# Second attention of a two-layer transformer kernel: router logits four tiles at a time with the gate matrix as weights, and the attention's gate multiplied into the projection's weights by GpSimd

## The reference

```
h  = layernorm(x) * (1 + ca) + sa                 # ca, sa, ga, cb, sb, gb: rows of 256 per batch
Q, K, V = (h @ Wq.T), (h @ Wk.T), (h @ Wv.T)      # 16 heads of 16
scores[b, s] = Q[b, s] @ K[b, s].T / 4            # 16 x 16: heads against heads of the same token
attn = softmax(scores);  o = attn @ V
x  = x + ga * (o @ Wfc.T)                         # ga: one row of 256 per batch
h  = layernorm(x) * (1 + cb) + sb
logits = h @ Wg                                   # Wg: 256 x 8 experts; then softmax, top tokens per expert
```

## Time and profile before

| | us |
|---|---|
| median of three runs | 1049.5 |
| lowest and highest run | 1048.51, 1049.79 |
| span of the profiled execution, first to last instruction | 1045.7 |
| second attention in it, first to last scores (L1713) | 553 to 777 |
| its tail until the router starts | until 822 |

### The profile page before, as it was taken

One profiled execution on the slowest core, in us unless ns is written; L12 is line 12 of the kernel. 1 busy time (PEld: TensorE's weight loads), 2 busy tenths in 40 slices (PEclk: granted clock), 3 DMA queues, 4 the chain that ended last, 5 costly groups with the idle time before them and its releaser, 6 DMA issues. The chain is left out here.

```text
span 1045.7 us, 30362 instructions
## 1 busy us (share of the span) xinstructions
PE 959.2 (92%) x11177; PEld 823.6 (79%) x11178; DVE 690.6 (66%) x1747; ACT 496.8 (48%) x1343; POOL 377.1 (36%) x330
## 2 busy tenths in 40 slices
PE   6899999889999999999987999999767888999996
PEld 3466666879999999999965778888666878899995
DVE  3478877855777777777412688889985776344442
ACT  3556665404454554554446777777552440322221
POOL 0134335521223223222213455555561101455552
PEclk9999999999999999999998899999868999999998
DMA  9885581294232222221055657766421620444441
GB/s 338 216 331 122 126 269 41 97 386 115 85 102 79 87 97 85 89 92 71 8 107 92 115 124 150 154 134 128 99 68 57 266 108 22 151 134 140 134 136 35
DMA packets 133025, 135.59 MB, mean 130 GB/s; under 512 B 73884, under 2 KB 122142, under 8 KB 130740
## 3 DMA queue, kind: packets, MB, share of 16 engines
q1 hardware_dynamic: 121684, 90.80, 31.5%
q0 software_dynamic: 11232, 43.27, 13.0%
HBM read 96.21 MB, written 44.77 MB: 135 GB/s over the span
## 5 line engine op out<-in xcount | busy, mean ns | idle before, releaser
L1151 PE MATMUL psall<-rows 128*128 128x128 f32 x1872 | 224.8, 277 | 1.6 <-issue 1.1
L1151 PEld LDWEIGHTS psall<-rows 128*128 128x128 f32 x1872 | 219.6, 194 | 3.1 <-issue 1.3
L1114 POOL DMA_INDIRECT x<-ffn_rows,tok_i x78 | 82.6, 1059 | 171.8 <-DVE tok_i L999 69.9
L1165 PE MATMUL psall<-whi,rows 128*128 x624 | 141.0, 379 | 0.0
L1244 DVE COPY rows<-wlo 128x2048 f32 (+2 forms) x78 | 74.5, 955 | 95.8 <-PE psall L1151 85.2
L1165 PEld LDWEIGHTS psall<-whi,rows 128*128 128x128 f32 x624 | 115.7, 190 | 14.1
L1119 POOL DMA_INDIRECT attn_rows<-rows,tok_i x39 | 41.7, 1070 | 183.9 <-DVE rows L1276 183.9
L1504 DVE STREAM_TRANSPOSE whi<-whi 32x512 f32<-32x512 f32 x128 | 89.7, 701 | 9.1 <-POOL whi L1467 7.7
L1584 ACT ACTIVATE whi<-psall 32x512 f32<-32x512 f32 x128 | 75.3, 588 | 30.8 <-PE psall L1713 27.3
L280 PE MATMUL psall<-cst 128*128 128x128 f32 x714 | 88.4, 280 | 0.5 <-PEq L1387 0.5
L1306 ACT ACTIVATE rows<-psall,vs 128x128 f32<-128x128 f32 x312 | 85.0, 383 | 4.4 <-PE psall L1151 2.1
(11 more groups left out here) (250 smaller groups left out, 1731.3 us busy)
## 6 DMA issues: line engine op xcount, KB each, us to landing
ffn_rows<-mod_rows SPq DMA_DIRECT2D x2, 4096.0 KB
wlo<-in_W SPq DMA_DIRECT2D x2, 4096.0 KB, 17.5
whi<-in_w SPq DMA_DIRECT2D x5, 1024.0 KB
whi<-mod_rows SPq DMA_DIRECT2D x4, 1024.0 KB, 15.0
ffn_rows<-rows SPq DMA_DIRECT2D x8, 512.0 KB
ffn_rows<-x SPq DMA_DIRECT2D x8, 512.0 KB
wlo<-attn_rows SPq DMA_DIRECT2D x32, 128.0 KB, 3.4
v_turn<-wlo SPq DMA_DIRECT2D x32, 128.0 KB, 2.6
```

Source lines behind the costliest of these rows:

```text
L1114: eng.indirect_dma_start(xin[j % DEEP], None, src_d, bass.IndirectOffsetOnAxis(tok_i[:, j:j + 1].bitcast(U32), 0), bounds_check=T, oob_is_ ...
L1151: last = eng.matmul(b_up[t.par][f // 4][:, (f % 4) * P:(f % 4 + 1) * P], w_now[:, c, f * P:(f + 1) * P], inT[t.par][:, c * P:(c + 1) * P], ...
L1165: last = eng.matmul(b_dn[t.par][:, 0:D], hidT[t.par][:, f * P:(f + 1) * P], w_down[:, bass.ds(e, 1), f, :].rearrange("p o n -> p (o n)"), ...
```

## The change

Logits: for all tiles but the last four, the logits are no longer computed tile by tile. When the four tiles of a batch have been turned, group_logits computes them with Wg as weights (8 columns wide, each tile in its own column group of the array) and the turned tiles moving; the result has experts as rows. ScalarE copies it in four pieces, TensorE turns it in the next step (turn_logits), and ScalarE copies it to where the router reads (keep_group_logits).

Gate: GpSimd multiplies `wfc` by the batch's row ga into a second copy `wfc_g`, in three parts in the three steps after the projection of the batch before (gate_weights). project uses `wfc_g` and waits for the parts by the semaphore `pre`. VectorE then adds its result to x for four tiles in one instruction; gate_attention, yb, the semaphore `ya` and GpSimd's additions are gone. SP loads ga as a row of its own (load_gate).

```diff
-        yb = cv(TB * D).rearrange("p (k d) -> p k d", d=D)
-        h1T = [cw(D) for _ in range(2 + TB)]
-        mod3 = [cw(3 * D).rearrange("p (j d) -> p j d", d=D) for _ in range(2)]
+        h1T = [cw(D) for _ in range(TB)]
+        mod2 = [cw(2 * D).rearrange("p (j d) -> p j d", d=D) for _ in range(2)]
+        cx = Carve(x)
+        wfc_g = cx(HH * D).rearrange("p (j n) -> p j n", j=HH)
+        gate_row = cx(D)
+        b_y4 = psall[:, 0:TB * 512].rearrange("p (k n) -> p k n", k=TB)[:, :, 0:D]
+        b_lgT, b_lgB = ps[6][:, D:D + P], ps[6][:, D + P:D + 2 * P]
...
 # SP
-                        for n, j in enumerate((GA, CB, SB_)):
+                        for n, j in enumerate((CB, SB_)):
...
+                def load_gate(t):
+                    b = t // TB
+                    if t % TB == 0:
+                        eng.wait_ge(ev["pre"], 3 * B + b)
+                        eng.dma_start(gate_row, mod_d[b:b + 1, (6 + GA) * D:(7 + GA) * D].broadcast_to([P, D])).then_inc(s_wb, 16)
...
-                tile_steps([(0, load_norm), (LAG_VST, store_v), (LAG_VLD, load_v), (LAG_XLD, load_x), (LAG_ROW, layer_rows),
+                tile_steps([(0, load_norm), (LAG_VST, store_v), (LAG_VLD, load_v), (LAG_XLD, load_gate), (LAG_XLD, load_x), (LAG_ROW, layer_rows),
                             (LAG_H, store_rows), (LAG_QK, turn_k)])
 # GpSimd
-                def add_attention(t):
-                    b, k = t // TB, t % TB
-                    eng.wait_ge(c_["ya"], b + 1)
-                    eng.wait_ge(s_x1[b % 2], 16 * (b // 2 + 1))
-                    eng.tensor_tensor(xr[b % 3][:, k, :], xr[b % 3][:, k, :], yb[:, k, :], ALU.add).then_inc(c_["xa"], 1)
-                tile_steps([(LAG_ET, normalize_exp), (LAG_X, add_attention), (LAG_MX, mask_other), (LAG_MX, sub_max)])
-                for t in LAST:
-                    add_attention(t)
+                def gate_weights(t):
+                    b, part = t // TB, t % TB
+                    if part == 0:
+                        eng.wait_ge(s_wa, 16 + 16 * (2 + TB))
+                        eng.wait_ge(s_wb, 48 + 16 * (b + 1))
+                        wait_some(eng, c_["y"], b)
+                    if part < 3:
+                        js = slice(3 * part, min(3 * part + 3, HH))
+                        last = eng.tensor_tensor(wfc_g[:, js], wfc[:, js], bc_mid(gate_row, js.stop - js.start), ALU.mult)
+                        if part == 2:
+                            last.then_inc(ev["pre"], 1)
+                tile_steps([(LAG_ET, normalize_exp), (LAG_MX, mask_other), (LAG_MX, sub_max), (LAG_Y, gate_weights)])
 # VectorE
-                def gate_attention(t):
+                def add_attention(t):
                     b = t // TB
                     if t % TB == TB - 1:
                         eng.wait_ge(c_["y"], b + 1)
-                        eng.wait_ge(s_m3[b % 2], 48 * (b // 2 + 1))
-                        wait_some(eng, c_["xa"], TB * b)
-                        for k in range(TB):
-                            last = eng.tensor_tensor(yb[:, k, :], b_y[k], mod3[b % 2][:, 0, :], ALU.mult)
-                        last.then_inc(c_["ya"], 1)
+                        eng.wait_ge(s_x1[b % 2], 16 * (b // 2 + 1))
+                        eng.tensor_tensor(xr[b % 3], b_y4, xr[b % 3], ALU.add).then_inc(c_["xa"], 1)
...
-                    eng.wait_ge(c_["xa"], t + 1)
+                    eng.wait_ge(c_["xa"], t // TB + 1)
...
 # ScalarE
+                def keep_turned_logits(t):
+                    if t % TB == TB - 1:
+                        eng.wait_ge(c_["lg"], 2 * (t // TB) + 1)
+                        for k in range(TB):
+                            last = eng.activation(affT[QD * k:QD * k + E, :], b_lgT[QD * k:QD * k + E, :], ACT.Copy)
+                        last.then_inc(c_["key"], 1)
+                def keep_group_logits(t):
+                    b = t // TB
+                    if t % TB == TB - 1:
+                        eng.wait_ge(c_["lg"], 2 * b + 2)
+                        eng.activation(key3[:, b * TB:(b + 1) * TB, :], b_lgB.rearrange("p (k n) -> p k n", k=TB)[:, :, 0:E], ACT.Copy
+                                       ).then_inc(c_["key"], 1)
...
-                tile_steps([(LAG_MX, compact((0, 1), False)), (LAG_N, shift_h), (LAG_V, keep_v), (LAG_EX, exps), (LAG_MX, compact((2, 3), True)),
-                            (LAG_H, keep_h1T), (LAG_QK, keep_qk), (LAG_PV, keep_oT), (LAG_H, keep_logits), (LAG_X, rstd2)],
+                tile_steps([(LAG_MX, compact((0, 1), False)), (LAG_N, shift_h), (LAG_H + 1, keep_group_logits), (LAG_V, keep_v), (LAG_EX, exps), (LAG_MX, compact((2, 3), True)),
+                            (LAG_H, keep_h1T), (LAG_QK, keep_qk), (LAG_PV, keep_oT), (LAG_H, keep_turned_logits), (LAG_X, rstd2)],
...
 # TensorE, project
+                        eng.wait_ge(ev["pre"], 3 * B + t // TB + 1)
-                                last = eng.matmul(b_y[k], oT[at, j, :], wfc[at, j, :], start=j == 0, stop=j == HH - 1)
+                                last = eng.matmul(b_y[k], oT[at, j, :], wfc_g[at, j, :], start=j == 0, stop=j == HH - 1)
...
+                def group_logits(t):
+                    if t % TB == TB - 1:
+                        eng.wait_ge(c_["h1T"], t + 1)
+                        wait_some(eng, c_["key"], 2 * (t // TB) - 1)
+                        for c in range(C):
+                            for k in range(TB):
+                                last = eng.matmul(b_lgT[QD * k:QD * k + E, :], wg[:, c, :], h1T[k][:, c * P:(c + 1) * P], start=c == 0, stop=c == C - 1)
+                        last.then_inc(c_["lg"], 1)
+                def turn_logits(t):
+                    if t % TB == TB - 1:
+                        eng.wait_ge(c_["key"], 2 * (t // TB) + 1)
+                        eng.transpose(b_lgB, affT, ident).then_inc(c_["lg"], 1)
...
-                    wait_some(eng, c_["ya"], done_by(t, LAG_S, LAG_Y) // TB)
+                    wait_some(eng, c_["xa"], done_by(t, LAG_S, LAG_Y) // TB)
...
-                tile_steps([(LAG_N, turn_n), (LAG_V, values), (LAG_QK, queries_keys), (LAG_H, turn_h), (LAG_PV, hold_last), (LAG_PV, weigh),
-                            (LAG_H, logits), (LAG_S, scores)],
+                tile_steps([(LAG_H + 1, turn_logits), (LAG_N, turn_n), (LAG_V, values), (LAG_QK, queries_keys), (LAG_H, turn_h), (LAG_PV, hold_last),
+                            (LAG_PV, weigh), (LAG_H, group_logits), (LAG_S, scores)],
```

More of the change, by code:

```diff
@@ L1356, in two_layer_kernel @@
         b_h = [bank[:, 0:D] for bank in (ps[6], ps[6], ps[4], ps[5], ps[1], ps[2])]
-        b_lg = [bank[:, D:D + E] for bank in (ps[6], ps[6], ps[4], ps[5], ps[1], ps[2])]
+        b_lg = [bank[:, D:D + E] for bank in (ps[4], ps[5], ps[1], ps[2])]
+        b_lgT, b_lgB = ps[6][:, D:D + P], ps[6][:, D + P:D + 2 * P]
         b_pv, b_v = ps[7][:, 0:D], ps[7][:, D:2 * D]
@@ L1523, in norm2 @@
                 def norm2(t):
-                    m3 = mod3[t // TB % 2]
+                    m2 = mod2[t // TB % 2]
+                    eng.wait_ge(s_m3[t // TB % 2], 32 * (t // TB // 2 + 1))
                     h, (_, mean, rstd) = one_of(h1, t), one_of(ln2, t)
@@ L1621, in _ @@
                         keep_logits(t - 1)
+                    else:
+                        keep_group_logits(t - 1)
                 keep_logits(NT - 1)
@@ L1634, in turn_n @@
                     wait_some(eng, c_["hT"], t)
-                    wait_some(eng, c_["key"], done_by(t, LAG_N, LAG_H, 1))
+                    wait_some(eng, c_["h1T"], done_by(t, LAG_N, LAG_H, 1))
+                    wait_some(eng, c_["key"], 2 * (done_by(t, LAG_N, LAG_H, 1) // TB) - 1)
                     for c in range(C):
@@ L1674, in turn_h @@
                     if t < FIRST_LAST:
-                        wait_some(eng, c_["key"], t)
+                        wait_some(eng, c_["h1T"], t)
+                        wait_some(eng, c_["key"], 2 * (t // TB))
                     for c in range(C):
@@ L1694, in weigh @@
                     last.then_inc(c_["pv"], 1)
+                def group_logits(t):
[10 more added lines that the diff above has]
+                        eng.transpose(b_lgB, affT, ident).then_inc(c_["lg"], 1)
                 def logits(t):
                     eng.wait_ge(c_["h1T"], t + 1)
-                    if t < FIRST_LAST:
-                        wait_some(eng, c_["key"], t)
                     for c in range(C):
-                        last = eng.matmul(one_of(b_lg, t), one_of(h1T, t)[:, c * P:(c + 1) * P], wg[:, c, :], start=c == 0, stop=c == C - 1)
+                        last = eng.matmul(b_lg[t - FIRST_LAST], h1T[t % TB][:, c * P:(c + 1) * P], wg[:, c, :], start=c == 0, stop=c == C - 1)
                     last.then_inc(c_["lg"], 1)
@@ L1721, in hold_last @@
                         hold_clock(eng, 12, b_unread)
-                tile_steps([(LAG_N, turn_n), (LAG_V, values), (LAG_QK, queries_keys), (LAG_H, turn_h), (LAG_PV, hold_last), (LAG_PV, weigh),
```

(9 more changed lines are left out.)

23 lines of the change are left out of this document (11 added, 12 removed).

## The result

The changed kernel takes 1077.95 us (median of 4 runs, 1077.15 to 1078.05) against 1049.01 us before in the same session: a ratio of 1.028, 95% interval 1.0263 to 1.0297. Forecast were 1081 us and a range of 1064 to 1095. The span of the profiled execution went from 1045.7 to 1076.1 us.

A forecast was written before the change was run, and what follows sets the result against it. VectorE with GpSimd, not TensorE, was taken to set the second attention's pace. Six batches +28.6, first batch +3.5, end -0.7 make +31.4 us on the 1045.7 us span, 1077.1, plus 3.8 carried over: 1081, range 1064 to 1095.

The forecast's parts named there:

- GpSimd: Second attention: multiplications between subtraction and next normalization lengthen three intervals between maxima by 1.82, 1.82 and 1.27, +4.91 us a batch.
- the collision: norm2's two-tensor VectorE instruction and GpSimd's instruction hold each other off; multiplication 0.18 us longer, 0.36 us per step, 6 us in all.
- First batch: Three parts where norm2 doesn't run yet: 0.5, 1.82 and 1.27 us added, with -0.15 for the addition, +3.5 us.
- VectorE's addition: At the projection step, one 1024-column addition from PSUM replaces four gatings: 1.2 instead of 1.36 us, -0.15 a batch.
- fourth intervals: Time between two starts of the maximum with the projection between them, one a batch: 9.59 us before, forecast near 9.4.
- the projection's wait for the weights: Projection waits for the third multiplication, ending 3.2 us after its marker; 2.4 us of cover, so cost 0.
- ScalarE's copies: Four logit copies in one step, 1.1 us instead of 0.18, ahead of the scores' copies: hidden; without cover 0.4 us a batch.
- The end: After the last maximum: one addition for four tiles, no GpSimd additions before statistics, later 1/sqrt; -0.7 us, between -1.5 and +0.5.
- The carried-over 3.8 us: Median 1049.5 us lies 3.8 us above the profiled span of 1045.7; added to the forecast span of 1077.1, giving 1081.
- TensorE as the bound: Rival 1: TensorE sets the pace, so its savings gain about 1.9 us a batch, -13 us, 1036; chance 0.07.
- The hidden case: Rival 2: GpSimd's multiplications don't delay the normalization; -2 us, 1047.7; chance 0.06.
- The fallen clock: Rival 3: forecast plus a low TensorE clock at the projection, fourth intervals 11 us or more; +8 us, 1089; chance 0.11.

The follow-up runs named there:

- the moved kernel: Changed kernel with GpSimd's three multiplications issued behind the normalization and ahead of the mask instead of last in the step: 1048.77 us, ratio 1.0007 to the kernel before.
- the narrow one: Changed kernel with 256 columns in each of the three multiplications instead of 768, 768 and 512, same place: 1064.66 us, ratio 1.0163 to the kernel before.

## Why the prediction was right

*What bounds the kernel.* Right, and shown from both sides: the logits part, which takes some 1.5 us a batch from TensorE (four steps of 0.61 us against one of 0.62 and one of 0.33; forecast 1.6), gains nothing by itself (1.0019, and 1.0002 with 1/sqrt first), and 1.3 to 1.8 us laid into VectorE's and GpSimd's chain appear one for one.

*GpSimd.* The price of a multiplication was taken from a line through two rows, 1.82 and 1.27 us, plus 0.18 for the collision; measured 1.80 to 1.83 and 1.26 to 1.27 alone, 1.98 to 2.01 and 1.44 to 1.45 beside norm2. Intervals: worked out 8.44, 8.44, 7.89, measured 8.40 to 8.45, 8.38 to 8.41, 7.84 to 7.85. Six batches: 29.5 us without the addition's share forecast, 28.7 found. First batch: 3.65 and 3.52. That the place and not the load costs is shown by the moved kernel; that it goes with the length by the narrow one. VectorE's wait before the first transpose was forecast as 1 to 1.6 us and is 0.94.

*The collision.* L1543 ends 0.28 us behind the multiplication's end and the normalization is again 1.23 us, as forecast; in the first batch, where norm2 doesn't run, the third part takes 1.27 instead of 1.45. Without the collision terms the sum would have been 6 us lower, some 5 under what was measured.

*VectorE's addition.* Forecast 1.2 instead of 1.36 us, measured 1.16 to 1.23. The fourth intervals gained 0.6 us in six, forecast 0.9, but that they come so near is luck. Forecast for each was 0.15 us less: 9.44 in batches 2 to 4. The gate part alone has 9.43 to 9.44 there; the changed kernel has 9.76, 9.59 and 9.73, and in batch 1 9.99 instead of 9.72. What these four lost is made up by batch 6, which gained 0.85 us on an interval that a slow projection (5.98 us) had lengthened to 10.04 us in the kernel before.

*TensorE* at 0 and the projection's wait for the weights at 0: right to within some 0.3 us a batch. TensorE does wait for the third part (12.6 us over five projections); in batches 3 to 5 it is through before VectorE's addition all the same. In batches 1 and 2 the addition waits for the projection:

```profile
609.72 1.23 DVE L1526 TENSOR_TENSOR wlo<-psall,wlo 128x1024 f32<-128x1024 f32 x1 [0.44 <-PE psall L1697]
...
644.16 1.23 DVE L1526 TENSOR_TENSOR wlo<-psall,wlo 128x1024 f32<-128x1024 f32 x1 [0.22 <-PE psall L1697]
```

There the projection doesn't wait for the weights; TensorE comes to it late, at a granted clock of 0.57 and 0.53 in the 8 us before. So what was priced too low in the fourth intervals is the clock: in batches 1 and 2 ahead of the projection, in batch 4 behind the longer wait for the addition, as shown with the projection interval above.

*ScalarE's copies.* The four take 1.11 us as estimated. Priced at 0 under the cover of longer intervals: that held in the changed kernel, where the wait lies under GpSimd's multiplication. Without cover I said 0.4 us a batch and looked only at the scores' copies; the logits-only kernel shows up to 1.7 us in a first interval, the larger part of it by way of 1/sqrt and norm2 and the rest by way of the scores' copies. What the forecast lacked is the second engine that waits behind the copies.

*The end.* Forecast -0.7, measured -1.3.

*The carried-over 3.8 us* between span and median was too much: the profiled execution took 1077.92 us with a span of 1076.1. That is 1.8 us around the span; the rest of the 3.8 would then be the difference between one execution and the median. It is two thirds of the 3 us by which the forecast was high.

*Rivals.* TensorE as the bound is out for this kernel. The hidden case was one line of order away. The fallen clock shows in parts: a clock of 0.95 in batch 3, 0.70 and 0.65 from 771 to 806 us, and the last three projections that wait for the weights are drawn out to 5.4, 6.6 and 6.8 us. But the fourth intervals are 8.4 to 10.0 us, not the 11 or more of the rival; it cost up to 0.3 us in some batches. TensorE's busy share in a batch is 85%, where the forecast had some 80%.

## What to carry to other kernels

Look for the engine whose instructions close a ring with another's, not for the busiest: here 6.6 us of maximum, subtraction, normalization and transposes turned around two engines at 90% and 60% busy. Work that is put on the less busy engine cost nothing here behind its last instruction of the ring, and within it what its length has over the slack of its place (0.2 us at the last place of the step), so it is placed by looking at what each slot of the engine's order waits for, in every kind of step. And a part that frees the engine which isn't the bound has to be measured alone, since its own side effects (here four small copies ahead of a 1/sqrt and of the scores' copies) may be all that it brings.

## What the runs showed of the hardware

A GpSimd multiplication with one operand repeated over the column groups takes 2.1 ns a column from 0.72 us for 256 columns to 1.27 for 512 and 1.82 for 768. A VectorE instruction with two tensors from SBUF that is issued while such a GpSimd instruction runs takes what is left of it plus 0.28 us: 0.48 us became 1.93. VectorE's addition with one operand in PSUM ran beside GpSimd's subtraction and normalization in 1.16 us, and the normalization took 1.05 us there, not the 1.23 that it takes beside norm2. TensorE's granted clock was 0.69 to 0.71 in 3.5 us behind a wait of 2.1 us, and its four passes of values took 1.91 us instead of 1.03. The four copies of 8 partitions by 128 columns on ScalarE took 1.11 us together, where one copy of 128 partitions by 512 columns took 0.60.
